# Two stacked cross-attentions on one core: PSUM banks by group, the last projection on four tiles, an exponential kept in SBUF, and new engine orders

## What is computed

```python
def _cma(x1, x2, ...):                      # layer 0, once per context: ctx_512 (a) and fside (v)
    x1n, x2n = _ln(x1, ln1_g, ln1_b), _ln(x2, ln2_g, ln2_b)
    q, k, v = x1n @ Wq + bq, x2n @ Wk + bk, x2n @ Wv + bv
    attn = softmax(einsum('bqe,bke->bqk', q, k) * scale)
    return einsum('bqk,bke->bqe', attn, v) @ Wo + bo
output = out_a + out_v + text
x = _ln(output, ln_g, ln_b) @ fc_W + fc_b + output
Q, K, V = x @ Wq + bq, ctx @ Wk + bk, ctx @ Wv + bv          # layer 1
x = x + softmax(Q @ K.T * scale) @ V @ Wo + bo
```

## Time and profile before

| | us |
|---|---|
| median of 3 runs | 189.41 |
| lowest, highest | 189.36, 191.41 |
| profiled execution | 190.28 |
| its span, first to last instruction | 188.1 |
| busy: TensorE, VectorE, ScalarE, GpSimd | 170.8, 148.8, 139.3, 122.4 |
| mean granted TensorE clock, share of full | 0.957 |

### The profile page before, as it was taken

One profiled execution on the slowest core, in us unless ns is written; L12 is line 12 of the kernel. 1 busy time (PEld: TensorE's weight loads), 2 busy tenths in 40 slices (PEclk: granted clock), 3 DMA queues, 4 the chain that ended last, 5 costly groups with the idle time before them and its releaser, 6 DMA issues.

```text
span 188.1 us, 6593 instructions
## 1 busy us (share of the span) xinstructions
PE 170.8 (91%) x2338; PEld 126.1 (67%) x2338; DVE 148.8 (79%) x561; ACT 139.3 (74%) x390; POOL 122.4 (65%) x248
## 2 busy tenths in 40 slices
PE   6957879999989999999999999999999999999742
PEld 6734658848666786777686778685878687676321
DVE  6998996999999999998579669466776969955531
ACT  3566834988988969969898886996988667565740
POOL 6468988688989998898797989995526132022000
PEclk9999855999999999999999999999999999999985
DMA  4999994001000200022200220111102201010121
GB/s 149 388 300 311 378 384 183 5 2 31 3 0 3 84 5 2 13 77 85 87 0 5 85 87 0 58 32 44 43 14 75 85 4 57 2 59 2 56 99 73
DMA packets 8882, 15.87 MB, mean 84 GB/s; under 512 B 1233, under 2 KB 1490, under 8 KB 8850
## 3 DMA queue, kind: packets, MB, share of 16 engines
q1 hardware_dynamic: 8562, 15.31, 23.9%
q10 hardware_dynamic: 288, 0.14, 0.3%
HBM read 11.25 MB, written 4.19 MB: 82 GB/s over the span
## 4 chain that ended last, share of the span: by engine, by line
PE 63%; DVE 28%; issue 4%; ACT 3%; POOL 2%; ACTq 0%; DVEq 0%; POOLq 0%
PE ps_d L1462 7%; PE ps_p L1447 6%; PE ps_d L1476 5%; PE ps_z L1406 5%; PE ps_g L1511 5%; PE ps_r L1486 4%; DVE stats L927 4%; PE ps_g L1437 4%; PE ps_p L1426 4%; PE ps_d L1470 4%; DVE stats L934 4%; PE ps_s L1416 3%; PE ps_s L1397 3%; PE ps_r L1455 3%; PE ps_s L1503 3%
## 5 line engine op out<-in xcount | busy, mean ns | idle before, releaser
L394 POOL TENSOR_TENSOR rstd<-st_var,minus_half 128x12 f32<-128x12 f32 x14 | 31.9, 2280 | 0.2 <-DVE stats L934 0.2
L620 ACT ACTIVATE z_sb<-x_sb,shift,rstd 128x128 f32<-128x128 f32 x64 | 26.4, 489 | 1.7 <-POOL shift L351 1.6
L1052 DVE SCALAR_TENSOR_TENSOR x_sb<-ps_d,rstd,res_sb 128x128 f32<-128x128 f32 x64 | 17.9, 343 | 7.5 <-PE ps_d L1462 6.6
L683 ACT ACTIVATE ps_r<-ps_r,minus_max 128x64 f32<-128x64 f32 x64 | 18.4, 289 | 2.3 <-DVE minus_max L1060 2.2
L452 POOL TENSOR_TENSOR rstd<-v_var,minus_half 128x4 f32<-128x4 f32 x7 | 7.1, 1009 | 19.5 <-DVE v_var L1044 19.5
L1462 PE MATMUL ps_d<-w_fc,resT_sb 128*128 128x128 f32 x128 | 18.5, 288 | 0.0
L1406 PE MATMUL ps_z<-zT_sb,m 128*128 128x512 f32 x32 | 17.4, 626 | 0.9 <-ACT zT_sb L627 0.7
L1447 PE MATMUL ps_p<-w,mix_sb 128*128 128x128 f32 x128 | 18.2, 287 | 0.0
L1447 PEld LDWEIGHTS ps_p<-w,mix_sb 128*128 128x128 f32 x128 | 16.7, 200 | 2.1 <-issue 1.5
L934 DVE BATCH_NORM_STATS2 stats<-cf_sb 128x6 f32<-128x64 f32 x128 | 17.5, 211 | 0.0
L1476 PE MATMUL ps_d<-x1T_sb,m 128*65 128x512 f32 x32 | 16.7, 602 | 0.0
(11 more groups left out here) (156 smaller groups left out, 444.0 us busy)
## 6 DMA issues: line engine op xcount, KB each, us to landing
x_sb<-in_x SPq DMA_DIRECT2D x16, 256.0 KB, 5.4
cf_sb<-in_cf SPq DMA_DIRECT2D x16, 256.0 KB, 5.7
out<-out_sb SPq DMA_DIRECT2D x16, 256.0 KB, 2.0
ct_sb<-in_ct SPq DMA_DIRECT2D x16, 128.0 KB, 2.8
w_sb<-in_w SPq DMA_DIRECT2D x1, 384.0 KB
w_score_sb<-in_w_score ACTq DMA_DIRECT2D x1, 128.0 KB, 2.9
w_sb<-in_w SPq DMA_DIRECT2D x1, 128.0 KB, 3.4
wt_sb<-in_wt SPq DMA_DIRECT2D x1, 96.0 KB
```

What stands on the lines that cost most here:

```text
L394: pool.tensor_tensor(rstd0[:, slot, :], st_var[:, g % SLOTS, :], minus_half[:, :], ALU.pow).then_inc(rstd0_done, 1)
L620: last = nc.scalar.activation(z_sb[:, g % Z_SLOTS, p, :], x_sb[:, g, p, :], ACT.Identity, bias=shift0[:, slot, p:p + 1], scale=rstd0[:, sl ...
L683: last = nc.scalar.activation(ps_r[:, p * S:(p + 1) * S], ps_r[:, p * S:(p + 1) * S], ACT.Exp, bias=minus_max1[:, slot, p:p + 1], accum_ou ...
L1052: last = v.scalar_tensor_tensor(x1_sb[:, g % SLOTS, p, :], ps_d[:, p * D:(p + 1) * D], rstd1[:, g % SLOTS, p:p + 1], res_sb[:, g % RES_SLO ...
```

## The change

1. **Banks.** The six named tensors become one, `ps` with eight banks, and each step of each group is given a bank number (steps with two banks, the number of the first). The waits for a bank's last reader are written only where other waits don't cover them.
2. **out1** runs as sixteen products of 64x64 tiles with 64 moving columns, in the same four-tile order as `mix0`.
3. **softmax1** writes its exponential to a new SBUF tile `exp1`, which `probs1` reads; it waits for `prob1_done` in place of `rsum1_done`.
4. **Orders** of TensorE, ScalarE, VectorE and GpSimd are written anew. Late folds come before `t0(0)`, `keep_busy(6)` goes, `stats_x(0)` comes before `score_affines`; the early variances get semaphores of their own; the two copies into `m0` become one. SyncE's order stays.

```diff
-        ps_z = bank("ps_z", [P, 512])
-        ps_s = bank("ps_s", [P, 2, 512])
...
+        ps = ctx.enter_context(nc.psum_tensor("ps", [P, 8, 512], F32))
+        exp1 = sb("exp1", [P, SLOTS, PAIRS, S])
...
-                need(act, rsum1_done, g - SLOTS + 1)
+                need(act, prob1_done, g - SLOTS + 1)
                 for p in range(PAIRS):
-                    last = nc.scalar.activation(ps_r[:, p * S:(p + 1) * S], ps_r[:, p * S:(p + 1) * S], ACT.Exp,
+                    last = nc.scalar.activation(exp1[:, slot, p, :], ps[:, bank, p * S:(p + 1) * S], ACT.Exp,
                                                 bias=minus_max1[:, slot, p:p + 1], accum_out=sum1[:, slot, p:p + 1])
...
-                v.tensor_tensor(prob1[:, g % SLOTS, :, :], by_pair(ps_r[:, 0:PAIRS * S]),
+                v.tensor_tensor(prob1[:, g % SLOTS, :, :], exp1[:, g % SLOTS, :, :],
...
+            def after(*reads):
+                for sem, count in reads:
+                    pe.wait_ge(sem, count)
...
-            def out1(g, sem, count):
+            def out1(g, bank, *reads):
                 pe.wait_ge(mix1_copied, g + 1)
-                bank_read(sem, count)
-                for u in range(DUOS):
-                    last = mm(ps_g[:, u, 0:2 * P], w1[HALF[u], :], mix1_sb[HALF[u], g % SLOTS, :, :, :],
-                              start=True, stop=True)
+                after(*reads)
+                for v in range(2):
+                    for b in range(2):
+                        at = (2 * v + b) * S
+                        for u, m in TILES:
+                            last = mm(ps[HALF[m], bank + u, at:at + S], w1[HALF[u], HALF[m]],
+                                      mix1_sb[HALF[u], g % SLOTS, v, b, :], start=True, stop=True)
                 last.then_inc(out1_made, 1)
```

TensorE's order at the start, around group 6, and at the end, before and after:

```diff
-            keep_busy(8)
-            score_folds_1()
-            score_folds_2()
-            keep_busy(6)
-            zT(0, zT_copied, 0)
-            t0(0, zT_copied, 1)
-            cfT(0, folds_copied, upto("m0_v"))
-            late_folds_1()
-            zT(1, t0_copied, 1)
-            s0(0, cfT_copied, 1)
-            t0(1, zT_copied, 2)
-            cfT(1, diff0_done, 1)
-            late_folds_2()
...
+            keep_busy(8, 7)
+            score_folds_1(0)
+            late_folds_1(2)
+            score_folds_2(3)
+            zT(0, 0)
+            late_folds_2(1)
+            t0(0, 0)
+            fold_bq1(2)
+            cfT(0, 3)
+            zT(1, 1, (late_folds_copied, upto_late("w1")))
+            s0(0, 4)
+            t0(1, 3)
...
-            mix1(4, prob1T_copied, 5)
-            s1(5, resT_copied, 7)
-            dense(6, t1_copied, 6)
-            cfT(9, mix1_copied, 5)
-            zT(10, t0_copied, 10)
-            out0(7, prob0T_copied, 8)
-            out1(4, mix0_copied, 8)
...
+            mix1(4, 0)
+            s1(5, 3)
+            mix0(7, 4, (diff0_done, 10))
+            out1(4, 0)
+            mix0(8, 6)
+            cfT(10, 2, (x1T_copied, 7))
+            t1(6, 0, (final_done, 5))
+            prob0T(9, 1)
+            out0(7, 2, (cfT_copied, 11))
...
-            dense(15, t1_copied, 15)
-            s1(14, resT_copied, 16)
-            mix1(13, prob1T_copied, 14)
-            x1T(15, x1_done, 16)
-            out1(13, final_done, 13)
-            t1(15, x1T_copied, 16)
-            prob1T(14, mix1_copied, 14)
-            s1(15, prob1_done, 15)
-            mix1(14, prob1T_copied, 15)
-            out1(14, final_done, 14)
...
+            dense(15, 1)
+            x1T(14, 2)
+            s1(13, 0)
+            mix1(12, 4)
+            out1(11, 2, (x1T_copied, 15))
+            out1(12, 4)
+            x1T(15, 1)
+            t1(14, 6)
+            prob1T(13, 0, (exp1_done, 14))
+            t1(15, 1)
+            s1(14, 2, (final_done, 12))
+            mix1(13, 4, (final_done, 13))
+            s1(15, 3)
+            out1(13, 0)
+            prob1T(14, 2, (exp1_done, 15))
+            mix1(14, 0, (final_done, 14))
+            prob1T(15, 2)
+            out1(14, 0)
+            mix1(15, 2, (exp1_done, 16))
+            out1(15, 2)
```

VectorE's order at the start, GpSimd's, and ScalarE's:

```diff
+            stats_x(0)
             score_affines()
-            stats_x(0)
             early_variance_x(0)
...
-            early_cfn(1)
-            max_scores0(0)
-            diff_scores0(0)
-            stats_x(3)
-            stats_cf(3)
-            sum_exp0(0)
-            stats_x(4)
-            stats_x(5)
-            recip_sum0(0)
-            stats_cf(4)
-            probs0(0)
...
+            stats_x(3)
+            early_cfn(1)
+            stats_cf(3)
+            max_scores0(0, 4)
+            diff_scores0(0, 4)
+            stats_x(4)
+            max_scores0(1, 2)
+            sum_exp0(0)
+            recip_sum0(0)
+            probs0(0)
...
             early_rstd_x(0)
             early_shift_x(0)
+            early_rstd_x(1)
+            early_shift_x(1)
             early_rstd_cf(0)
...
-            copy_early_folds_2()
             z(0)
-            copy_zT(0)
-            z(1)
+            copy_late_folds_1(2)
+            copy_zT(0, 0)
+            copy_early_folds_2(3)
+            z(1)
+            copy_late_folds_2(1)
...
+            softmax1(14, 2)
+            softmax1(15, 3)
```

More of the change, by code:

```diff
@@ new lines, in _ @@
+            out0(3, 2)
+            s1(1, 0, (t0_copied, 6))
+            mix1(0, 4)
+            s0(5, 2, (res_done, 4))
+            resT(3, 1, (x1T_copied, 3))
+            zT(6, 6)
+            cfT(6, 7)
+            dense(3, 1)
+            t0(6, 6)
+            prob0T(4, 7, (cfT_copied, 7))
+            t1(2, 0, (exp1_done, 2))
+            prob1T(1, 6, (t0_copied, 7))
+            out1(0, 2, (diff0_done, 6))
+            s0(6, 4)
+            mix1(1, 0, (t1_copied, 3), (x1_done, 4))
+            mix0(4, 6)
@@ new lines, in _ @@
+            s1(2, 2, (final_done, 1))
+            x1T(3, 3)
+            out1(1, 0)
+            cfT(7, 4, (diff0_done, 7))
+            zT(7, 3, (x1T_copied, 4))
+            out0(4, 5)
+            prob0T(5, 4, (cfT_copied, 8))
+            t0(7, 3)
+            resT(4, 5)
+            t1(3, 2, (exp1_done, 3))
+            prob1T(2, 3, (t0_copied, 8))
+            dense(4, 0, (final_done, 2))
+            prob0T(6, 1)
+            s1(3, 2)
+            mix1(2, 4, (prob0T_copied, 6))
+            s0(7, 6)
@@ new lines, in _ @@
+            mix0(5, 4, (mix1_copied, 3))
+            zT(8, 1, (prob0T_copied, 7))
+            x1T(4, 0)
+            cfT(8, 2, (exp1_done, 4))
+            t0(8, 1)
+            prob1T(3, 0, (x1T_copied, 5))
+            t1(4, 2, (cfT_copied, 9))
+            out0(5, 0, (prob1T_copied, 4))
+            mix1(3, 4)
+            out1(2, 6, (diff0_done, 8))
+            s0(8, 2, (t1_copied, 5))
+            mix0(6, 0, (res_done, 6))
+            out1(3, 4)
+            resT(5, 6, (final_done, 3))
@@ new lines, in _ @@
+            dense(8, 0, (prob1T_copied, 6))
+            zT(11, 3, (exp1_done, 6))
+            mix1(5, 4, (exp1_done, 7))
+            s0(10, 6)
+            mix0(9, 2, (zT_copied, 12))
+            out1(5, 4)
+            prob1T(6, 1, (x1_done, 8))
+            x1T(7, 2, (mix0_copied, 10))
+            t0(11, 3)
+            x1T(8, 0)
+            cfT(11, 1, (prob1T_copied, 7))
+            out0(9, 2, (x1T_copied, 8))
+            t1(7, 0, (x1T_copied, 9))
+            resT(9, 1, (cfT_copied, 12))
@@ new lines, in _ @@
+            t1(8, 2)
+            s1(7, 3, (t0_copied, 12))
+            mix1(6, 0, (resT_copied, 10))
+            s0(11, 4, (final_done, 6))
+            dense(9, 6, (diff0_done, 11))
+            prob0T(10, 2, (t1_copied, 9))
+            zT(12, 7)
+            s1(8, 3, (exp1_done, 8))
+            out1(6, 0)
+            mix0(10, 4, (diff0_done, 12))
+            prob1T(7, 2)
+            t0(12, 6, (x1_done, 10))
+            x1T(9, 3, (exp1_done, 9))
+            cfT(12, 2, (prob1T_copied, 8))
@@ new lines, in _ @@
+            t0(13, 2, (final_done, 8))
+            prob1T(9, 3)
+            x1T(10, 0, (final_done, 9))
+            out0(11, 1)
+            prob0T(12, 2, (t0_copied, 14))
+            t1(10, 0)
+            resT(11, 1)
+            zT(14, 3, (prob1T_copied, 10))
+            s1(10, 0)
+            mix1(9, 4)
+            s0(13, 6)
+            mix0(12, 2, (zT_copied, 15))
+            out1(9, 4)
+            dense(11, 1)
+            t0(14, 0, (exp1_done, 11))
+            prob1T(10, 2, (mix0_copied, 13))
@@ new lines, in _ @@
+            cfT(14, 3)
+            out0(12, 4, (final_done, 10))
+            x1T(11, 2, (prob1T_copied, 11))
+            mix1(10, 0, (t0_copied, 15))
+            s0(14, 6, (diff0_done, 14))
+            resT(12, 3)
+            zT(15, 4)
+            cfT(15, 5)
+            dense(12, 2, (x1T_copied, 12))
+            prob0T(13, 3)
+            t0(15, 0, (mix1_copied, 11))
+            t1(11, 1)
+            x1T(12, 2)
+            s0(15, 4)
+            mix0(13, 0, (t1_copied, 12))
```

(16 more changed lines are left out.)

1414 lines of the change are left out of this document (639 added, 775 removed).

## The result

The changed kernel took 183.16 us (median of 4 runs, 181.77 to 184.14) where the kernel before took 190.41 in the same comparison: ratio 0.961, 95% interval 0.951 to 0.971. The same kernel measured again (after_again) took 182.38 us, 0.959 (0.954 to 0.965). The forecast was 182.2. The profiled execution took 181.77 us with a span of 179.6, so 8.5 us less span than before (forecast 7.2). It is the shortest of its four; by the medians the gain is 7.3 and 7.9 us.

What follows compares the result with a forecast made beforehand. TensorE was taken as the bound from 62 to 173 us, VectorE first from 31 to 62. Terms -7.0 + 0 + 0.5 - 2.5 - 1.4 + 3.2 = -7.2 us, from 189.41 to 182.2 us; range 177 to 186.

Steps and rivals of the forecast that it cites:

- Visits to tiled products: TensorE's orders: 29 fewer changes from full-size to tiled steps, at 0.24 us each, -7.0 us.
- out1 on four tiles: out1 on TensorE as sixteen 64x64 products: worth nothing alone, 0 to -0.3 us over 16.
- exp1 in SBUF: Softmax 1: slower ScalarE exponentials, +0.2 us in the tail, and VectorE divisions meeting GpSimd, +0.3; +0.5 us together.
- The start: Before the long stretch: late folds delay s0(0) by 1.5 us, shorter centring and less VectorE waiting gain; -2.5 us, bounds +2, -4.
- the wrong sign: Start: s0(0) past 19 us would show the start term wrong.
- The tail: After dense(15): 3.4 us of TensorE work moves into idle time, against +2.0 for softmax1(14) and t1 copies; net -1.4 us.
- New waits: New tiled pairs on TensorE: eight waits for copies not ready, about 0.4 us each, +3.2 us, bounds 0 and +10.
- rival (b): In-order waits inside the 29 new tiled pairs on TensorE; at 0.5 us each +4.1, 193.5 us; chance 0.08.
- (a): Rival: VectorE and ScalarE take TensorE's place as bound, leaving -1.2 us, 188.2 us; chance 0.10.
- a wrong sign: VectorE over 95% busy past 62 us would speak for VectorE and ScalarE taking TensorE's place.
- (c): Rival whose sign is a second stretch at half clock; size not given in the text; chance 0.08.
- (d): Rival: softmax 1 divisions on VectorE collide with GpSimd, a third of 16 at 1.06 us, +5.6, 186 us; chance 0.04.

Runs made afterwards that it cites:

- out1_wide: Changed kernel with out1 put back to two 64x128 products of 256 columns, orders kept: 181.22 us, ratio 0.955.
- before_exp1_sbuf: The kernel before with only the exp of softmax 1 written to an SBUF tile: ratio 1.000 (0.995 to 1.004).
- the run with fillers: Changed kernel with five keep_busy products behind out1(13) and one behind prob1T(14), in the tail: 181.67 us, ratio 0.956.
- kernels of mine: Changed kernel with all late folds behind s0(1): 186.68 us; changed kernel with eight fillers and a new order of the last steps: 186.58 us.
- the control: Changed kernel with 35 small full-size products put ahead of full-size steps that follow full-size steps: 184.51 us, ratio 0.971.

## Why the prediction was right, point by point

The total was right (182.2 against 183.16 and 182.38) and so was the mechanism that carries it. That it came within 1 us is in part luck: the start and the tail gave some 2.4 us less than forecast, the visits and the new waits about as much more. The upper end of its range, 186, doesn't follow from its bounds either: start, tail and waits at their worst add up to 197. Of its terms:

- **Visits to tiled products, -7.0: right.** Busy time fell by 6.1 us although the start ran at half clock (its busy time rose from 22.17 to 25.12). One break costs 0.24 to 0.28 us on the trace, and 35 of them 7.7 at the end. The price was a little short in one part: the first tiled step behind a full-size one takes 0.05 more than one behind a tiled step (0.52 for 0.47), beside the 0.05 of the full-size step behind the visit that is in the 0.24. So "0.52 start to start" came out as 0.46 to 0.49 inside a run. By 29 visits at 0.04 to 0.05 the term was an estimated 1.2 to 1.5 us too small. (Up to x1T(1) the written orders have 7 and 6 visits, not "6 and 5"; the 29 stay.)
- **out1 on four tiles, 0: right**, and the part in the visit count that it "buys" never reached the end (out1_wide). By the spacing of starts that the Trainium skill gives (TensorE: Matmul & The Clock Gate, "Wait — 56ns, not 53.3ns?": about 25 ns) it would lose 2.6 us. The trace contradicts this again: 32 instructions in 0.46 us inside a run are under 15 ns each.
- **exp1 in SBUF, +0.5: right** within 0.9 us; the division's share was mis-sized (+0.3, measured +0.9 to +1.1 of VectorE time).
- **The start, -2.5: wrong.** The step that failed is "I put s0(0) 1.5 us later": it came 4.7 later and past the 19 us named as the wrong sign. The centring did fall from 2.33 to 0.21 us, but nothing came of it: it stands behind stats_x(0), which waits for x until 3.54 us, so the scaling that the folds need ends later than before and the first fold starts at 6.09 us in place of 5.43. And I had priced eleven late folds at "about 0.3 us each", the rate of full clock, 3.4 us in all; here they take 2.46 us (from 8.91 to 11.37) and 3.51 (from 12.97 to 16.48), 6.0 in all. Here the half-clock stretch lies on them (in the old-out1 run's record 0.50 from 9.5 to 19.2 us with TensorE busy throughout), where it had lain on a fuller stretch, 21.9 to 32.1 us. That pays the loss back: dense(0) starts at 34.21, 0.8 us earlier than before. So the term was -0.8, with both halves of the reasoning off, and even the -0.8 may be the clock's alone: in before_exp1_sbuf, with the old start, the half clock lay from 12.1 to 22.3 us and dense(0) came at 33.94. The three runs that moved the folds or added fillers brought nothing or made it worse.
- **The tail, -1.4: about half.** The 3.4 us moved behind dense(15), which came at 160.85 ("near 162"), and TensorE's idle time there fell. But the +2.0 of the new order is +2.7: 16.1 us from dense(15) to the end before, 18.75 after. The clock accounts for it: half clock began 9.1 us before the end, where the 0.81 over 15.10 us of the earlier trace rows works out at 5.7 us before, and the run with fillers puts its price at 1.6 us. Without it the new order would have cost about 1 us against the old tail, which had its own half clock.
- **New waits, +3.2: too large.** TensorE's idle time from 31 to 164 us grew by 2.1, but 1.1 of it are the two stalls, which the prediction didn't have, so the waits for other engines grew by 1.0. None of them is long (the longest is 0.8 us), so rival (b) didn't happen by itself. It happened twice in kernels of mine, at 5.3 and 4.2 us.
- **Rivals.** (a) shows in part: VectorE is busy 32.26 of 33 us from 62 to 95 us, which the prediction had named as a wrong sign, and it is why the control's 6 us of further TensorE time cost only some 2. It did not take the gain. (c) didn't happen in the long stretch. (d) is there, in three of the 16 (0.49, 0.55 and 1.28 us). A GpSimd bound, in no rival, stands in the chain with 13% and is worth nothing in the profile and at most some 1.7 us by the medians.

## What to carry to other kernels

Price a step on TensorE from start to start, once inside a run of its own shape and once alone: the difference, times the visits that a new order removes, was good to a sixth here, and a dummy product between steps against the same one elsewhere measures it directly. Before moving a step, follow every wait of what stands behind it on all engines, buffer slots included; the two kernels in which one was overlooked lost 4 to 5 us, more than any of these moves could gain. An engine's share of the chain is not what it would give back: taking away 30 us of GpSimd's work cut its share from 13% to 2% and moved the end by nothing in the profile and by 1.0 to 1.7 us in the medians.
